# A graph-attention edge loop of 26 rounds, written out on all five engines

## The reference

```python
x = x + gnn(layernorm(x), edge_attr_16, edge_attr_4, ...)      # x: 6250 nodes x 256
x = x + ffn(layernorm(x)[None], ...)[0]                        # 8 experts, 2 of them for each node
# gnn: 200000 edges, sorted by their target node, 8 heads of 32, 4 mask values
feat_src = (feat @ W_n).reshape(N, H, D)
left  = einsum('eht,et->eh', el[src], mask)                    # el, er: products of feat_src
right = einsum('eht,et->eh', er[dst], mask)
e = (left + right + em_e) / 3.0
e = where(e > 0, e, 0.2 * e)
a = softmax of e over the edges of one target node
rst = segment_sum(feat_src[src] * a[:, :, None], dst)
```

## Time and profile before

| | |
|---|---|
| median of 3 runs | 4229.73 us (4228.48 to 4230.96) |
| the profiled execution | 4242.61 us |
| its span, first to last instruction | 4240.8 us |
| instructions in the trace | 66247 |
| mean granted TensorE clock | 0.771 |
| busy | PE 74%, DVE 47%, POOL 44%, ACT 38% |

### The profile page before, as it was taken

The page is one execution under the profiler, slowest core; times in us unless marked ns, Lnnn a source line. Parts: engine busy times, 40 slices in busy tenths (PEclk is TensorE's granted clock), DMA queues, the critical chain, the costliest instruction groups (busy, mean ns, idle before and its releaser), DMA issues. The chain is left out here.

```text
span 4240.8 us, 66247 instructions
## 1 busy us (share of the span) xinstructions
PE 3155.8 (74%) x12650; PEld 2393.4 (56%) x12651; DVE 1982.3 (47%) x5336; ACT 1615.5 (38%) x3611; POOL 1861.5 (44%) x1906
## 2 busy tenths in 40 slices
PE   2532787777777777777777777777766699999997
PEld 1221665555565656555555665565555477777775
DVE  5730555555555555555555555555744122222221
ACT  2311544444444444444444444444422122222221
POOL 0005455556555555555555555555245111111111
PEclk9865667777767777777777677767755899999998
DMA  7744444444444444444444444446553321221113
GB/s 217 253 134 120 122 128 124 125 127 126 125 125 127 128 123 127 131 128 126 125 127 124 125 125 125 125 125 118 87 176 133 101 32 30 32 31 31 31 31 82
DMA packets 311626, 480.40 MB, mean 113 GB/s; under 512 B 164215, under 2 KB 239811, under 8 KB 302670
## 3 DMA queue, kind: packets, MB, share of 16 engines
q0 software_dynamic: 100848, 285.40, 27.4%
q1 hardware_dynamic: 208606, 193.39, 15.2%
q10 hardware_dynamic: 2000, 0.06, 0.0%
HBM read 408.92 MB, written 76.12 MB: 114 GB/s over the span
## 5 line engine op out<-in xcount | busy, mean ns | idle before, releaser
L838 POOL DMA_INDIRECT rows<-table,idx x1664 | 1577.9, 948 | 1141.0 <-issue 488.8
L881 PE MATMUL ps_acc<-rows,hot 128*128 128x264 f32 x3328 | 1274.3, 521 | 396.9 <-DVE acc L1169 342.9
L881 PEld LDWEIGHTS ps_acc<-rows,hot 128*128 128x128 f32 x3328 | 767.9, 255 | 535.1 <-issue 422.0
L1169 DVE TENSOR_TENSOR acc<-acc,ps_acc 128x264 f32 x832 | 356.7, 429 | 1047.0 <-remote 459.5
L866 PEld LDWEIGHTS ps_term<-er,hot_t 128*128 128x128 f32 x3328 | 619.1, 249 | 285.6 <-issue 235.6
L866 PE MATMUL ps_term<-er,hot_t 128*128 x3328 | 608.2, 314 | 125.6 <-issue 93.3
L1155 DVE TENSOR_TENSOR rows<-rows,ps_p 128x512 f32<-128x512 f32 x832 | 565.7, 680 | 2.4 <-ACT ps_p L984 0.5
L973 ACT ACTIVATE hot<-iota_row,neg_rel 128x128 f32<-128x128 f32 x1664 | 545.8, 388 | 4.8 <-PE ps_acc L881 4.6
L1713 PE MATMUL ps_h<-w,acc 128*128 x1680 | 530.8, 459 | 0.5 <-ACT acc L1632 0.5
L1625 POOL DMA_INDIRECT x_dram<-acc,to x105 | 161.8, 1541 | 755.2 <-ACT acc L1641 755.2
L948 ACT COPY e_t<-ps_e 128x128 f32<-128x128 f32 x208 | 57.5, 277 | 1003.1 <-remote 684.3
(11 more groups left out here) (264 smaller groups left out, 2960.7 us busy)
## 6 DMA issues: line engine op xcount, KB each, us to landing
dst_row<-rel_d SPq DMA_DIRECT2D x52, 1024.0 KB
rows<-table,idx POOLq DMA_INDIRECT x1664
rec<-rec_d SPq DMA_DIRECT2D x848, 24.0 KB
rec_d<-acc SPq DMA_DIRECT2D x16, 1050.0 KB
acc<-slots_x SPq DMA_DIRECT2D x105, 130.0 KB, 2.1
acc<-in_edge_attr_dram SPq DMA_DIRECT2D x16, 700.0 KB
wrow<-in_L_ffn_w_dram SPq DMA_DIRECT2D x16, 640.0 KB
table<-fo SPq DMA_DIRECT2D x49, 148.0 KB
```

Source lines behind the costliest of these rows:

```text
L838: pool.indirect_dma_start(rows[w][:, t, :], None, table, bass.IndirectOffsetOnAxis(ap=idx[w][:, t:t + 1], axis=0)).then_inc(gathered[w * Q ...
L881: last = pe.matmul(ps_acc[m % 2][:, 0:PW], hot[m // QI % 2][:, m % QI * G + j, :], rows[m // NI][:, tile_of(m % NI, j), 0:PW], start=(j == ...
L1169: dve.tensor_tensor(so_far, so_far, ps_acc[m % 2][:, 0:PW].rearrange("p (h d) -> p h d", h=HEADS), ALU.add).then_inc(added, 1)
```

## The change

`all_slots` runs all rounds from -1 to 26 in a Python loop, so that `i` is a number everywhere. The register forms of `Steps` go, and so do the 16 more entries of `start_i` and the record loads of the 53rd batch. The order of the work on each engine stays.

```diff
-PER_ROUND = 2 * (2 * QUADS + 10)
...
     def __call__(self, ins):
         ins.then_inc(self.sem, 1)
-        self.n += 1
-        if self.per is None:
-            self.base += 1
-            self.n = 0
-            self.eng.wait_ge(self.sem, self.base)
-        else:
-            self.eng.wait_ge(self.sem, self.i * self.per + (self.start - self.first * self.per + self.n))
+        self.base += 1
+        self.eng.wait_ge(self.sem, self.base)
...
-        start_i = sb(edges_ctx, "start_i", [1, ITEMS + NI], I32)
+        start_i = sb(edges_ctx, "start_i", [1, ITEMS], I32)
...
-            def all_slots(body, eng, steps=None):
-
-                for i in (-1, 0):
-                    for w in range(2):
-                        body(i, w)
-                with eng.Fori(1, ROUNDS - 1) as i:
-                    if steps:
-                        steps.loop(i, PER_ROUND, 1)
-                    for w in range(2):
-                        body(i, w)
-                if steps:
-                    steps.end(ROUNDS - 2)
-                for i in (ROUNDS - 1, ROUNDS):
+            def all_slots(body):
+
+                for i in range(-1, ROUNDS + 1):
                     for w in range(2):
                         body(i, w)
...
                     load_records(0, 0)
-                    all_slots(slot, sp)
-                    sp.wait_ge(rec_in[0], 16 * NI * (BATCHES // 2 + 1))
+                    all_slots(slot)
+                    sp.wait_ge(rec_in[0], 16 * NI * (BATCHES // 2))
```

More of the change, by code:

```diff
@@ L87, in __init__ @@
     def __init__(self, eng, sem):
[L88 to L99, removed]
+        self.eng, self.sem, self.base = eng, sem, 0
     def __call__(self, ins):
         ins.then_inc(self.sem, 1)
-        self.n += 1
-        if self.per is None:
-            self.base += 1
-            self.n = 0
-            self.eng.wait_ge(self.sem, self.base)
-        else:
-            self.eng.wait_ge(self.sem, self.i * self.per + (self.start - self.first * self.per + self.n))
+        self.base += 1
+        self.eng.wait_ge(self.sem, self.base)
 def wait_apart(eng, sem, value, tick):
@@ L603, in _ @@
                                                            ALU.mult, ALU.add))
-                    dve_steps(dve.memset(start_i[:, ITEMS:ITEMS + NI], EDGES))
                     dve_steps(dve.tensor_scalar(start_i[:, 0:ITEMS], start_f[:, :], float(EDGES), None, ALU.min))
@@ L840, in slot @@
                                                             gathered[w * QUADS + u // QI], 16)
-                    all_slots(slot, pool)
+                    all_slots(slot)
                 @block.tensor
@@ L937, in slot @@
                                     (turn_scores, item_ends, carries, back)[u](i, w)
-                    all_slots(slot, pe)
+                    all_slots(slot)
                 @block.scalar
@@ L1032, in _ @@
                     act.wait_ge(e3_const, 1)
-                    all_slots(slot, act)
+                    all_slots(slot)
                 @block.vector
@@ L1202, in slot @@
                                         (item_tops, link, tops)[u - 1](i, w)
-                    all_slots(slot, dve, step)
+                    all_slots(slot)
         edges_ctx.close()
```

## The result

The change takes **4176.67 us** (4173.89 to 4178.57, 4 runs) against 4229.77 us (4228.48 to 4230.96): ratio 0.9874 (95% interval 0.9858 to 0.989), 53.1 us faster. 4168 was forecast.

A forecast was written before the change was run, and what follows sets the result against it. The prediction took engines waiting for each other in the edge loop as the bound. Branch 39 us plus register arithmetic 23 us made 62 us, so 4229.7 - 62 = 4168 us; its own range was 4114 to 4191, the full range 4110 to 4234.

The forecast's parts named there:

- What bounds the loop: Edge loop, some 2465 us: no engine is full; engines waiting for each other set the pace, 51.33 us a slot.
- rival 2: Edge loop: POOL's runs of gathers set the pace and nothing is gained, 4230 us; chance 0.12.
- The branch, 39 us: DVE's loop end: 23 taken branches at 1.7 us each are saved, 39 us; upper end 71 us.
- the long waits: DVE's add in the edge loop: "remote" waits of 4.6 us, two a slot, tied to POOL's gather runs; expected to stay.
- my upper end: Upper end for DVE's branch: 23 x 3.1 us, all of its standing time, 71 us.
- The register arithmetic, 23 us: Sequencer instructions per item on DVE and PE: 502 places at 0.09 us, 45 us, half taken; ends 0 and 45.
- The sum: Whole kernel: 39 + 23 = 62 us saved from the median 4229.7, giving 4168 us; chance 0.56.
- The other engines: SP, POOL and ACT in the edge loop: their removed instructions are hidden and gain nothing.
- Rival 3: Straight-line code: instruction fetches on the path, one a slot at 3.1 us, cost 146 us, giving 4314; chance 0.10.
- Rival 1: Edge loop: coupled slots give the branch's time back; only 23 us remain, 4207 us; chance 0.12.
- rival 4: Edge loop: one of four long waits in two slots goes, 108 us more, giving 4060; chance 0.10.
- What was to be seen: Signs: DVE's 3.1 us gap gone, slots near 50 us, add's "issue" waits about 120 us, long waits two a slot.

The follow-up runs named there:

- hint_dve: Kernel before with a prefetch hint on the back edge of DVE's loop alone: 3625.21 us, ratio 0.9896 to the kernel before, on another chip.
- the third group: Four kernels with the second gather of every other item left out (24 a slot for 32), lifting POOL's cap: 3635.09, 3541.24, 3476.21 and 3474.48 us.
- dve_alone: Kernel before with rounds 1 to 24 written out with constants on DVE only, other engines keeping their loops: 3623.22 us, ratio 0.9896.
- loop_dve: The change, but DVE keeps its loop with branch and register arithmetic: 3678.44 us, ratio 1.0036 to the kernel before.
- before_again: Kernel before, unchanged, run again for a trace on another chip: traced execution 3658.45 us; the kernel before there has median 3660.13 us.
- after_again: The change itself, unchanged, run on another chip: 3617.90 us, ratio 0.9882 to the kernel before.
- few_change: The change with 24 gathers a slot in place of 32: 3476.21 us, ratio 0.9498 to the kernel before with 32.
- few_before: Kernel before with 24 gathers a slot in place of 32, loop and register arithmetic kept: 3635.09 us, ratio 0.994 to the kernel before.
- few_early: The change with 24 gathers a slot, block numbers loaded one item ahead on PE and DVE: 3474.48 us, ratio 0.9483 to the kernel before with 32.

## Why the prediction was right or wrong

**What bounds the loop: right, and incomplete.** No engine is full on the chip of the first traces, and the waits set the pace. On the other chips POOL becomes the bound as soon as the change is made. There rival 2 (the runs of gathers set the pace) holds in part: it doesn't cancel the gain, it cuts it off at 40.0 us a slot, 42 us where with fewer gathers the same change gives 159.

**The branch, 39 us: mechanism right, size too small as a price.** That DVE alone stands 3.1 us, 23 times, and that a fetch at the target is what it waits for, hint_dve shows: with the branch announced to the fetch, and nothing else changed, the gap is gone. I took 1.7 us a branch from one pair of slots of the first trace; over its 47 slots the two kinds differ by 1.2 us on average. My reason was that some of the 3.1 us is made up within the slot. On chips without the long waits nothing is made up within the slot, it grows: 6.3 us, of which the next slot gives back a part. With the cap lifted, writing out all five loops gives 93.9 us; put down to DVE's 23 branches that is 4.1 us each, above my upper end, though the other engines' part in it was not tried. With the cap, 39 us come out for hint_dve, my number, but there POOL's rate cuts the gain off; that the two agree is luck.

**The register arithmetic, 23 us: the term with the weakest base, and its sign in the trace misread.** My bound was 45 us, 502 places by 0.09 us, for the adds' and products' idle time that ends in "issue". On the other chips it measures 0.2 us (3618.1 against 3617.9) under the cap and 65.0 without it, so neither the half nor the upper end carries over. The bound counted only the places that show as "issue" (and left out 18 of those, PE's at `ps_l`); in the third group most of what the arithmetic costs was in the add's waits for PE. That is the weak step. On the first chip its worth was not measured.

**The sum: near, with its two terms unproven.** On the first chip the change gave 53.1 us for 62 forecast. How these split there is open: no experiment ran on a chip that takes 4230 us. The trace leans to the branch: of the add's "issue" time 57 us went at the branch and 14 elsewhere, and the branch slots lost 39 us and the others 13. The slots of 50.23 us are as long as the one branch-free slot of the earlier trace rows (50.3), but the 24 branch-free slots of before average 50.74, so something was gained in them too. That the 39 and 13 stand so near my 39 and 23 proves neither term, since one kind of slot can give back what the other loses, as in the third group.

**The other engines: nothing, held in part.** dve_alone gives 36.9 of 42.2 us under the cap; the rest, 5.3 us, is near what the runs can tell. What any one engine's loop or arithmetic is worth without the cap was not tried apart. Why loop_dve is 14 us slower than the kernel before stays open: its slots without the branch last 38.63 us on average, against 38.11 in before_again, and those with it the same 44.0 and 44.1.

**Rival 3, fetches on the path: fell.** The packets are 265 (89 + 176) for 172. The change is faster, and on the chips without long waits no idle gap of DVE in the slots of after_again reaches 2 us; few_change keeps all 47 slots between 37.4 and 38.0 us. On the first chip DVE has five "issue" gaps of 1.9 us or more in the slots, where before had none but the branch's; what they are isn't known, and they are too few for this rival. The Trainium skill's "Runtime: NRT & Kernel Launch", section Instruction fetch mechanics, says that sequential code is fetched ahead; the trace agrees.

**Rival 1 (the branch's time is given back) and rival 4 (a long wait in four goes): fell.** The gain, 53 us, lies far from rival 1's 23 and rival 4's 170. Of the add's waits, 75 "remote" ones are left of 93, but those for PE grew from 193 to 234; as counted above, the long ones only changed their name.

**What was to be seen.** The gap is gone and the slots are alike: right (50.23 for 50.0). The add's "issue" waits at 120 us: 146, too high by 26. The long waits at two a slot: right. POOL's waits for `acc_done` shrank by 67 us (546 to 480) where the slots shrank by 52. The stages behind are 5 us shorter, 1293.4 for 1298.4.

## What to carry to other kernels

A long loop can pay a fetch of code at its back edge on one engine only; look for a gap between the branch and the next instruction in each engine's queue, and try the prefetch hint there first: one line gave 39 us, where writing out 24 rounds on five engines gave 42, both with POOL as the cap. Without the cap the hint was not tried. A stall in an engine that takes turns with another isn't priced by its own length, nor by the "issue" time alone: 3.1 us became 6.3 by the end of the slot, and of the 65 us that the register arithmetic cost only 25 were in the add's "issue" waits. Where an experiment says that an edit is worth nothing, first ask what rate the kernel now stands at; 40.0 us was 32 gathers at 1.25, and with that lifted the same edit was worth 65 us.

## What the runs showed of the hardware

**The same kernel takes 4230 us on one chip and 3660 on three others.** Of the spans' difference, 4240.8 - 3656.7 = 584 us, 503 are in the 51 slots (51.0 against 41.1 each), 64 ahead of the first slot's end and 17 behind the last. The gathers are as fast on both (a gather's median is 947 and 946 ns). But the first chip's records show small sequencer instructions with far more scattered times. SP's line L790, which reads the start of a record, ns min/median/max, first the chip of 4230 us:

```profile
L790 SPq TENSOR_LOAD <-start_i x848: 2/267/1430, 293.2 to 2916.2; - x170
L790 SPq SEQ_ASSERT  x848: 2/18/1412, 293.9 to 2916.7; - x170
```

and before_again:

```profile
L790 SPq TENSOR_LOAD <-start_i x848: 262/267/479, 291.6 to 2351.4; - x170
L790 SPq SEQ_ASSERT  x848: 18/18/37, 292.4 to 2351.9; - x170
```

The same instruction of 18 ns takes up to 1412. Part of this may be the records' own times and not the work: loads as short as 2 ns stand there too, and the 848 loads add up to 231 us on the first chip and 229 on the other. The "remote" waits of DVE's add, 93 in the earlier trace rows, do not exist in before_again. The kernel is the same, so both come with the chip or its state at the time; what makes them was not found. A change's worth in us carries over between such chips only roughly: 53 and 42.

**Fewer packets with the hint.** I had expected the same fetches, only earlier. The queue shows 5 packets a round fewer (39 for 154), those in mid-round too, and no gap; whether the hint's own fetches are left out of the records, the runs don't show.

**The clock did not set the pace.** In the 47 slots the granted clock is 0.79 in few_before, 0.82 in few_regs and 0.85 in few_change, whose slots get shorter in this order. But few_early has 0.82, PE at work for 1506 us in place of few_change's 1470, and the same time; the 36 us went into what had been PE's waits. On the first chip the slots got shorter too while the clock went the other way, 0.73 before and 0.71 of the change.
